# A graph layer's last softmax and tail: four guard passes on ScalarE, reciprocals cut in other pieces, a minimum of negated logits, far rows moved behind the second step's weights, tiles finished one after the other

## What is computed

```python
h = relu(layernorm(x))                                   # x is 256 x 1024
e = relu(concat(h[src], h[dst]) @ W_kind + b_kind)       # 8448 edges, three kinds of edge
logit = (e @ W_a + b_a)[:, 0]
alpha = softmax of logit over the edges with the same dst
z = segment_sum(alpha[:, None] * h[src], dst)
x = x + relu(concat(h, z) @ W_hn + b_hn)   for rows 0..63
x = x + relu(concat(h, z) @ W_on + b_on)   for rows 64..255
h2 = relu(layernorm(x))
out = x + h2 @ W.T + bias      # W: edge_weight added up at (src, dst), only its 256 x 256 corner is not zero
```

## Time and profile before

| | us |
|---|---|
| median of 3 runs (lowest, highest) | 320.19 (319.69, 320.27) |
| the profiled execution, its own time | 319.85 |
| its span in the trace | 317.8 |
| TensorE busy in the span | 306.4 (96%) |
| VectorE, ScalarE busy | 255.8 (81%), 174.4 (55%) |

### The profile page before, as it was taken

How to read it: one execution, slowest core, us unless ns; L and a number is a source line. 1 busy time by engine, 2 the same in 40 slices (tenths; PEclk the granted TensorE clock), 3 DMA queues, 4 the chain that set the end, 5 groups by cost and what they waited for, 6 DMA issues and landing times.

```text
span 317.8 us, 4204 instructions
## 1 busy us (share of the span) xinstructions
PE 306.4 (96%) x1394; PEld 194.1 (61%) x1399; DVE 255.8 (81%) x442; ACT 174.4 (55%) x437; POOL 154.5 (49%) x149
## 2 busy tenths in 40 slices
PE   8899999999979899999999999999999998999995
PEld 3687688656646667566566666575744645456443
DVE  4775448490799999999979999979898798998164
ACT  3892351573067775648966655865338675493102
POOL 3140027305877778778757877468778600000000
PEclk9999999999999999999999999999999999999999
DMA  6999999999999999999999999999999999999604
GB/s 194 418 425 416 399 427 366 419 424 415 402 405 411 410 407 414 411 410 412 419 419 406 413 415 407 418 418 410 413 413 413 411 414 411 395 377 426 244 0 132
DMA packets 29384, 122.04 MB, mean 384 GB/s; under 512 B 3498, under 2 KB 4010, under 8 KB 24628
## 3 DMA queue, kind: packets, MB, share of 16 engines
q0 software_dynamic: 19008, 69.21, 54.5%
q1 hardware_dynamic: 9236, 48.38, 38.1%
q10 hardware_dynamic: 1120, 4.19, 3.2%
HBM read 115.49 MB, written 6.29 MB: 383 GB/s over the span
## 4 chain that ended last, share of the span: by engine, by line
PE 51%; DMA 20%; DVE 10%; POOL 8%; issue 6%; ACT 4%; SPq 0%; DVEq 0%; ACTq 0%; POOLq 0%
PE psG L1086 17%; PE psG L959 14%; DMA Gp<-p_ho,ids 9%; PE psA L996 5%; DMA q_ho<-T 4%; PE psW L996 4%; POOL Gq L428 3%; DMA q_oo<-T 3%; DVE Gp L737 3%; POOL Gp L414 3%; DMA Gq<-q_ho,ids 2%; PE psG L1163 2%; PE psB L996 2%; PE psG L1056 2%; ACT RL L547 2%
## 5 line engine op out<-in xcount | busy, mean ns | idle before, releaser
L1086 PE MATMUL psG<-W,hT 128*128 128x512 f32 x192 | 84.9, 593 | 0.0
L414 POOL DMA_INDIRECT Gp<-p_ho,ids x60 | 64.1, 1068 | 42.5 <-DMA p_ho<-T 21.4
L737 DVE TENSOR_TENSOR Gp<-Gp,Gq 128x1024 f32<-128x1024 f32 x57 | 69.6, 1220 | 16.6 <-DMA Gq<-q_ho,ids 11.1
L428 POOL DMA_INDIRECT Gq<-q_ho,ids x56 | 65.9, 1178 | 31.3 <-issue 16.8
L741 DVE SCALAR_TENSOR_TENSOR Gp<-Gp,wa 128x1024 f32<-128x1024 f32 x65 | 79.2, 1219 | 0.6
L1086 PEld LDWEIGHTS psG<-W,hT 128*128 128x128 f32 x192 | 35.3, 190 | 39.1 <-issue 39.1
L537 ACT ACTIVATE RW<-ohs,ewh 128x256 fp32r<-128x256 f32 x66 | 33.1, 502 | 34.4 <-DVE ohs L728 28.4
L996 PE MATMUL psW<-RW,ohd 128*128 128x256 f32 x264 | 44.2, 290 | 0.0
L996 PE MATMUL psA<-RL,ohd 128*128 128x256 f32 x240 | 35.4, 291 | 4.3 <-ACT RL L547 3.7
L996 PEld LDWEIGHTS psW<-RW,ohd 128*128 128x128 f32 x264 | 36.3, 189 | 2.9 <-issue 2.9
L996 PEld LDWEIGHTS psA<-RL,ohd 128*128 128x128 f32 x240 | 30.4, 189 | 9.3 <-ACT RL L547 8.2
(11 more groups left out here) (187 smaller groups left out, 393.0 us busy)
## 6 DMA issues: line engine op xcount, KB each, us to landing
W<-weights SPq DMA_DIRECT2D x30, 1024.0 KB, 8.5
Gq<-weights SPq DMA_DIRECT2D x2, 1024.0 KB, 9.3
Gp<-weights SPq DMA_DIRECT2D x4, 512.0 KB, 8.7
Gp<-weights SPq DMA_DIRECT2D x2, 1024.0 KB, 11.8
xs<-x SPq DMA_DIRECT2D x4, 256.0 KB, 3.6
W<-weights SPq DMA_DIRECT2D x2, 512.0 KB, 6.7
h_rows<-h SPq DMA_DIRECT2D x1, 1024.0 KB, 9.0
pre_f<-weights SPq DMA_DIRECT2D x1, 1024.0 KB, 9.9
```

What stands on the lines that cost most here:

```text
L414: nc.gpsimd.indirect_dma_start(out=Gp[:, i % NP, :], out_offset=None, in_=p_oo if t <= OO_TILES else p_ho, in_offset=bass.IndirectOffsetOn ...
L428: nc.gpsimd.indirect_dma_start(out=q_place[Q_PLACE[i]], out_offset=None, in_=q_oo if t <= OO_TILES else q_ho, in_offset=bass.IndirectOffse ...
L737: nc.vector.tensor_tensor(Gp[:, i % NP, :], Gp[:, i % NP, :], q_place[Q_PLACE[i]], ALU.add).then_inc(s_sum, 1)
L1086: last = nc.tensor.matmul(psG[:, 2 * t + half, :], hT[:, k, t * P:(t + 1) * P], W[:, s, half * HALF:(half + 1) * HALF], start=u != 1 and k ...
```

## The change

- **Guards.** ScalarE makes a fourth pass, `inv` = -inv - 1, so that it holds the negated count, and VectorE's addition of 1 is gone. `off` gets the opposite sign with a negated bias tile `nbar`, made once at the start. `inv`, `off`, `Z` and `Ex` lie in `few` and `inv_few`, so the passes wait for `few_sums`.
- **Softmax.** `exp_in` takes the minimum of negated values straight into `nm[:, 1]`; the two small operations behind it are gone, and ScalarE works with scale -1 and with `mx` as a bias. Columns 0 to 63 of tile 1's reciprocal come before `exp_in(0)`, 64 to 127 behind it, 128 to 255 behind `alphas(0)` as before.
- **TensorE.** `keep_busy` ahead of `turned(0)` is gone. The eight `sums` lie in two banks and are copied in two passes. The loop of `hn_rows` and `on_rows` starts right behind them, with `turned(1)` inside it; then `far_rows(0)`, `swapped_stats`, `far_rows(1)`. In the tail, transpose and second layer of tile 0 come first, with two and five `keep_busy` matmuls around them, and then those of tile 1.
- **VectorE.** Tile 0's new rows and statistics come first, then tile 1's; tile 0's last addition (L898) stands ahead of both L895.
- **SP's queue.** x is loaded ahead of `brep`, tile 0's three parts first and tile 1 on a semaphore of its own. The order of the stores is as before.

```diff
 
-        _, inv, off, Z, Ex, zT = shared(("gq_low", [P, 1, D], f32), ("inv", [P, NT, N], f32),
-                                           ("off", [P, NT, N], f32), ("Z", [P, NT, N], f32), ("Ex", [P, NT, N], f32),
-                                           ("zT", [P, KC, NH], f32))
+        _, zT = shared(("gq_low", [P, 1, D], f32), ("zT", [P, KC, NH], f32))
         Gq = sb("Gq", [P, NQ, D], f32)
         RW = sb("RW", [P, WRING, 2, N], f32r)
         _, pre_l = shared(("rl_low", [P, D], f32), ("pre_l", [P, 2, D], f32))
@@ -205,9 +203,11 @@
         inv_few = sb("inv_few", [P, 2, NT, N], f32)
         L_few = sb("L_few", [P, 2, NT, N], f32)
         off_few = sb("off_few", [P, 2, NT, N], f32)
+        inv, off = few[:, 0, :, :], few[:, 1, :, :]
+        Z, Ex = inv_few[:, 0, :, :], inv_few[:, 1, :, :]
+        nbar = sb("nbar", [P, 1], f32)
         mx = sb("mx", [P, 2, NT], f32)
         nm = sb("nm", [P, 2, NT], f32)
-        ed = sb("ed", [P, NT], f32)
         fall = sb("fall", [P, NT], f32)
...
             for j in range(KC // 2):
                 load_hn(j)
-            sp.wait_ge(s_used, BREP_AT + 1)
-            sp.dma_start(brep, l1_bias.broadcast_to((P, D))).then_inc(s_lb, 16)
             sp.wait_ge(s_tab[2], 16)
             sp.wait_ge(s_sum, len(GATHERED))
-            sp.dma_start(x1[:, 1, :], x[P:N, :]).then_inc(s_xlo, 16)
             sp.dma_start(x1[:, 0, 0:HALF], x[0:P, 0:HALF]).then_inc(s_xlo, 16)
             for rows, place_of in ((lower, upper), (upper, lower)):
                 sp.dma_start(x1[place_of, 0, HALF:D], x[rows, HALF:D]).then_inc(s_xlo, 16)
+            sp.dma_start(x1[:, 1, :], x[P:N, :]).then_inc(s_xhi, 16)
+            sp.wait_ge(s_used, BREP_AT + 1)
+            sp.dma_start(brep, l1_bias.broadcast_to((P, D))).then_inc(s_lb, 16)
             sp.wait_ge(s_ylo, 1)
             sp.dma_start(out[0:P, N:HALF], x1[:, 0, N:HALF]).then_inc(s_out, 16)
             for rows, place_of in ((lower, upper), (upper, lower)):
...
             nc.scalar.copy(selr[:, :], sel[:, :]).then_inc(s_bh, 1)
+            nc.scalar.activation(nbar[:, :], bar[:, :], ACT.Copy, scale=-1.0).then_inc(s_bh, 1)
             highs(6, KC + 2)
...
             def guard_counts():
 
                 act.wait_ge(s_counted, ET)
-                act.wait_ge(s_sum, FREED_Q + 1)
-                nc.scalar.activation(inv[:, :, :], psC, ACT.Relu, bias=minus[:, 0:1]).then_inc(s_cm, 1)
-                nc.scalar.activation(off[:, :, :], psC, ACT.Relu, bias=unit[:, 0:1], scale=-1.0).then_inc(s_cm, 1)
+                act.wait_ge(s_fewsum, 1)
+                act.wait_ge(s_bh, 3)
+                nc.scalar.activation(inv, psC, ACT.Relu, bias=minus[:, 0:1]).then_inc(s_cm, 1)
+                nc.scalar.activation(off, psC, ACT.Relu, bias=unit[:, 0:1], scale=-1.0).then_inc(s_cm, 1)
                 act.wait_ge(s_cm, 2)
-                nc.scalar.activation(off[:, :, :], off[:, :, :], ACT.Identity, bias=bar[:, 0:1], scale=NEG).then_inc(s_cm, 1)
+                nc.scalar.activation(inv, inv, ACT.Identity, bias=minus[:, 0:1], scale=-1.0).then_inc(s_cm, 1)
+                nc.scalar.activation(off, off, ACT.Identity, bias=nbar[:, 0:1], scale=-NEG).then_inc(s_cm, 1)
 
             def lot_weights(g):
                 if LOTS[g][0] > OO_TILES:
@@ -619,14 +623,16 @@
             nc.scalar.copy(Wd[:, :, :], psW[:, :, :]).then_inc(s_Wd, 1)
             for c in range(NT):
                 act.wait_ge(s_ed, c + 1)
-                nc.scalar.activation(Ex[:, c, :], Z[:, c, :], ACT.Exp, bias=nm[:, 1, c:c + 1]).then_inc(s_ex, 1)
-                nc.scalar.activation(fall[:, c:c + 1], ed[:, c:c + 1], ACT.Exp).then_inc(s_fall, 1)
+                nc.scalar.activation(Ex[:, c, :], Z[:, c, :], ACT.Exp, bias=nm[:, 1, c:c + 1], scale=-1.0).then_inc(s_ex, 1)
+                nc.scalar.activation(fall[:, c:c + 1], nm[:, 1, c:c + 1], ACT.Exp, bias=mx[:, 0, c:c + 1]).then_inc(s_fall, 1)
                 if c == 0:
                     act.wait_ge(s_AT, 1)
                     nc.scalar.copy(AT[:, :, 0:P], psB[:, 1, 0:N].rearrange("p (j n) -> p j n", n=P)).then_inc(s_ATc, 1)
+            for part in range(2):
+                act.wait_ge(s_zT, part + 1)
+                nc.scalar.copy(zT[:, 4 * part:4 * part + 4, :],
+                               (psW[:, 0, :], psB[:, 1, 0:N])[part].rearrange("p (k n) -> p k n", n=NH)).then_inc(s_zTc, 1)
             nc.scalar.activation(warm[:, :], epst[:, :], ACT.Sqrt)
-            act.wait_ge(s_zT, 1)
-            nc.scalar.copy(zT[:, :, :], whole(psW).rearrange("p (k n) -> p k n", n=NH)).then_inc(s_zTc, 1)
             for n, t in enumerate(TAIL):
                 act.wait_ge(s_st2, n + 1)
                 nc.scalar.activation(sd[:, t:t + 1], mv[:, t, 1:2], ACT.Sqrt, bias=epst[:, 0:1]).then_inc(s_sd2, 1)
...
                 chain(nc.vector.tensor_tensor(L_few[:, :, :, :], L_few[:, :, :, :], few[:, :, :, :], ALU.mult))
-                chain(nc.vector.tensor_tensor(A[:, :, :], L_few[:, 0, :, :], L_few[:, 1, :, :], ALU.add))
+                nc.vector.tensor_tensor(A[:, :, :], L_few[:, 0, :, :], L_few[:, 1, :, :], ALU.add).then_inc(s_fewsum, 1)
...
             def exp_in(c):
 
                 chain(nc.vector.tensor_tensor(Z[:, c, :], psA[:, c, :], inv[:, c, :], ALU.mult))
-                chain(nc.vector.tensor_tensor_reduce(out=Z[:, c, :], in0=Z[:, c, :], in1=off[:, c, :], scale=1.0,
-                                                     scalar=mx[:, 0, c:c + 1], op0=ALU.add, op1=ALU.max,
-                                                     accum_out=mx[:, 1, c:c + 1]))
-                nc.vector.tensor_scalar(nm[:, 1, c:c + 1], mx[:, 1, c:c + 1], -1.0, None, ALU.mult)
-                nc.vector.tensor_tensor(ed[:, c:c + 1], mx[:, 0, c:c + 1], mx[:, 1, c:c + 1], ALU.subtract).then_inc(s_ed, 1)
+                nc.vector.tensor_tensor_reduce(out=Z[:, c, :], in0=Z[:, c, :], in1=off[:, c, :], scale=1.0,
+                                                     scalar=nm[:, 0, c:c + 1], op0=ALU.add, op1=ALU.min,
+                                                     accum_out=nm[:, 1, c:c + 1]).then_inc(s_ed, 1)
...
                 nc.vector.tensor_scalar(A[:, c, :], A[:, c, :], den[:, c:c + 1], None, ALU.mult).then_inc(s_alpha, 1)
 
             dve.wait_ge(s_cm, 3)
-            chain(nc.vector.tensor_scalar(inv[:, :, :], inv[:, :, :], 1.0, None, ALU.add))
+            dve.wait_ge(s_ef, 1)
+            dve.wait_ge(s_fewsum, 1)
             inverse(0, 0, N)
+            inverse(1, 0, NH)
+            dve.wait_ge(s_cm, 4)
             dve.wait_ge(s_placed, ET)
             exp_in(0)
-            inverse(1, 0, P)
+            inverse(1, NH, P)
             alphas(0)
             inverse(1, P, N)
             exp_in(1)
             alphas(1)
             dve.wait_ge(s_AT, 2)
             nc.vector.tensor_copy(AT[:, :, P:N], psB[:, 1, N:2 * N].rearrange("p (j n) -> p j n", n=P)).then_inc(s_ATd, 1)
-            dve.wait_ge(s_xlo, 16 * 4)
...
                 nc.vector.scalar_tensor_tensor(out=nb[:, t:t + 1], in0=mv[:, t, 0:1], scalar=-1.0,
                                                in1=rs[:, t:t + 1], op0=ALU.mult, op1=ALU.mult).then_inc(s_nb2, 1)
 
-            new_rows(1, 0)
-            chain(rows_stats(1, 0))
+            dve.wait_ge(s_xlo, 16 * 3)
             for half in range(2):
                 new_rows(0, half)
                 rows_stats(0, half).then_inc(s_stp, 1)
-            new_rows(1, 1)
+            dve.wait_ge(s_xhi, 16)
+            new_rows(1, 0)
+            rows_stats(1, 0)
             dve.wait_ge(s_sts, 1)
             nc.vector.bn_aggr(mv[:, 0, :], psS).then_inc(s_st2, 1)
+            norm2(0, 0)
+            new_rows(1, 1)
             chain(rows_stats(1, 1))
             nc.vector.bn_aggr(mv[:, 1, :], st[:, 1, :, :].rearrange("p b s -> p (b s)")).then_inc(s_st2, 1)
-            for n, t in enumerate(TAIL):
-                norm2(n, t)
+            norm2(1, 1)
+
+            def second_rows(n, t):
+                dve.wait_ge(s_y, n + 1)
+                nc.vector.tensor_tensor(x1[:, t, 0:N], x1[:, t, 0:N], (psW, psA)[t][:, 0, :], ALU.add).then_inc(s_o, 1)
+
+            second_rows(0, 0)
             dve.wait_ge(s_lb, 16)
             for t in TAIL:
                 nc.vector.tensor_tensor(x1[:, t, N:D], x1[:, t, N:D], brep[:, N:D], ALU.add).then_inc(s_ylo, 1)
-            for n, t in enumerate(TAIL):
-                dve.wait_ge(s_y, n + 1)
-                nc.vector.tensor_tensor(x1[:, t, 0:N], x1[:, t, 0:N], (psW, psA)[t][:, 0, :], ALU.add).then_inc(s_o, 1)
+            second_rows(1, 1)
 
         @block.tensor
         def _(pe):
...
                 for j in range(NT):
-                    ins = nc.tensor.matmul(whole(psW)[:, k * NH:(k + 1) * NH], rows_h[:, j, k * P:(k + 1) * P],
+                    ins = nc.tensor.matmul((psW[:, 0, :], psB[:, 1, 0:N])[k // 4][:, k % 4 * NH:(k % 4 + 1) * NH], rows_h[:, j, k * P:(k + 1) * P],
```

(31 more changed lines are left out.)

## The result

The changed kernel took 321.91 us (median of 6 runs, 320.34 to 323.94) against 319.68 us for the kernel before, a ratio of 1.0087 with a 95% interval of 1.0056 to 1.0118: +2.2 us. Forecast were 321.5 and +1.36. The direction was right, the size was not: 0.87% where 0.43% was said. The absolute time is only 0.4 us off because the kernel before came out 0.5 us under the median on record. The profiled execution took 321.78 us with a span of 319.8.

A forecast was written before the change was run, and what follows sets the result against it. Two paths were taken to end together: tile 1's final addition (+0.83 us) and SP's line of six stores (+1.36). The later path sets the end: 320.19 + 1.36, near 321.5 us, range 320.3 to 322.2, slower 0.80.

The forecast's parts named there:

- Guards and softmax: ScalarE's guard passes and the softmax: VectorE's placed logits 0.3 us later, yet `turned(0)` starts 0.13 us sooner.
- TensorE from the sums to `second_bias`: TensorE's reordered list: `sums` 3.8 us, loop 8.74 plus 0.6 for `turned(1)`, all ended at 310.0 against 310.06 before.
- From 306.7 is 309.8, an upper bound for one tile: Tile 0's `h2` done within 3.14 us of 306.7, so `h2_turned(0)` starts at 310.0, 1.43 us sooner.
- rival 4: TensorE's clock falls because `keep_busy` calls are gone; half clock from `turned(0)` on would cost many us; chance 0.01.
- The line of stores: SP's six last stores, released by the first L895, start 1.36 us later and move the end by that; chance 0.61.
- Rival 1: SP's line of stores doesn't bind; the end goes with tile 1's final addition, +0.83 us: 321.0; chance 0.13.
- two paths end together: In the kernel before, tile 1's final addition and the line of stores end together; delaying either moves the end.
- The rule on issuing time: At SP's stores the trace doesn't agree: six issues take 3.27 of the last 5.7 us; the rule would give Rival 1.
- Rivals 2 and 3: 2: `keep_busy` and stores hide in waits, 320.2, chance 0.12. 3: small TensorE matmuls cost no time, -2.1 us, 319.5, chance 0.08.

The follow-up runs named there:

- before_pause: Kernel before without its five `keep_busy` ahead of `h2_turned(0)`; 27.69 us from `turned(0)` to the end, against 26.98 in the kernel before.
- roots_apart: Changed kernel with ScalarE making tile 0's `h2` right behind tile 0's root, ahead of tile 1's root; ratio to the kernel before 1.0090.
- pause_filled: Changed kernel with five more `keep_busy` in front of `h2_turned(0)`, where TensorE was idle; ratio to the kernel before 1.0078.
- no_five: Changed kernel without the five `keep_busy` between tile 0's layer and `h2_turned(1)`; ratio to the kernel before 1.0096.
- tile_by_tile: Changed kernel with ScalarE doing root, `h2` and copy of tile 0, then of tile 1; ratio to the kernel before 1.0015 in the third run.
- bias_first: Changed kernel with both additions of `brep` ahead of tile 0's final addition, as in the kernel before; ratio to the kernel before 1.0056.
- pause_again: Second run of before_pause, the same kernel; 27.52 us from `turned(0)` to the end, against 26.98 in the kernel before.

## Why the prediction was right or wrong, point by point

- **Guards and softmax: right.** VectorE could go on with the placed logits 2.64 us behind its own last logit, against 2.35 before: +0.29, 0.3 forecast. `turned(0)` gained 6.30 - 6.12 = 0.18 on the same scale, 0.13 forecast. The minimum took 0.48 us as the maximum did, and alone the part is neutral (0.9994). x was in time too: VectorE's first new rows of tile 0 waited for TensorE, and came 2.1 us sooner behind `turned(0)` than before (12.30 against 14.40).
- **TensorE from the sums to `second_bias`: right, 0.3 to 0.4 us too dear.** The two halves of `sums` led from 290.49 to the loop in 3.71 us where I had 3.96. Loop with `turned(1)`: 9.25, forecast 9.2. `far_rows` 1.83, `swapped_stats` 0.42: as forecast. `second_bias` ended at about 308.7, 19.1 behind `turned(0)`; I had 19.4.
- **"From 306.7 is 309.8, an upper bound for one tile": the step that failed.** I took the stretch from `far_rows(1)` to both `h2` in the earlier trace rows as a bound and reasoned only with VectorE's order. On ScalarE tile 0's `h2` had to wait for tile 1's root, and the root for VectorE's new rows of tile 1, which wait for the *second* far group. From the end of the first far group (about 305.4) it took 4.8 us, not 3.14. With ScalarE's order mended in full the tail fell from 30.18 to 28.13, and from 29.68 where only the clock was held: 1.55 us for the order.
- **The clock: rival 4, given 1 in 100, was in the profile.** I priced the pause ahead of `turned(0)`, 0.1 to 0.4 us, and not one ahead of `h2_turned(0)`, since the step above had removed it. Cost in the profile 30.18 - 29.68 = 0.50 us. The Trainium skill, TensorE: Matmul & The Clock Gate, section Part 1: The HAM clock gate, has the clock follow the engine's recent activity; before_pause agrees, where it fell 0.5 us behind the end of a pause of 1.30 us.
- **The line of stores: right.** SP's six issues ran without a gap in roots_apart, pause_filled, no_five and tile_by_tile, and the end came 5.6 to 5.7 us behind the first, as it did in the kernel before (5.66) and in the changed one (5.59). Rival 1 is out: no_five's last addition was ready 0.87 us sooner than pause_filled's, and the end didn't move. But "two paths end together" was wrong of the kernel before: its end came 3.44 us behind the start of its last addition, where 2.65 to 2.74 are enough, so that path had 0.7 us or more to spare. before_pause agrees: the addition came 1.47 us later, the end 0.71.
- **The rule on issuing time: not settled.** The Trainium skill, DMA: Bandwidth & Descriptors, section Issuing engines are not separate DMA queues, calls the time to start a transfer usually small beside the transfer. The changed kernel's sixth store was issued 0.4 us late and took 0.33 us of SP's time, against 0.55 in no_five, and the end came no later behind the first store. So the 5.6 us of the line aren't SP's time alone, and no run here separates it from the transfers.
- **The size of the forecast: 0.4 us too dear even for the kernel that I had in mind.** In tails the forecast was 319.2 - 290.7 = 28.5; tile_by_tile has 28.13, and the interval of its time, -0.2 to +1.1 us, leaves out +1.36. Predicted mechanism 28.13 - 26.98 = 1.15, ScalarE's order 1.55, the clock 0.50: together the 3.2 us. That the measured 321.91 falls into the stated range of 320.3 to 322.2 is luck: +2.2 us on the 320.19 on record would be 322.4.
- **Rivals 2 and 3: out.** Moved matmuls kept their time (0.42 for `swapped_stats`, 1.06 for `second_bias` in pause_filled), and ten `keep_busy` took 1.1 us from their start to the next instruction's at full clock.

Open: the times agree with the tails only within about 0.7 us. Less the 0.2 us that `turned(0)` gained, the tails of roots_apart, pause_filled, no_five and bias_first ask for +3.3, +2.5, +2.5 and +1.1 us; the ratios give +2.9, +2.5, +3.1 and +1.8. That the clock falls behind the pause in other executions of no_five and bias_first than the profiled ones would explain their excess, but it wasn't counted over more traces. The clock's 0.50 us rests on single profiles. In the times, of the five edits of the tail that were made to find the cause, only tile_by_tile (1.0015) stands clear of the changed kernel (1.0087).

## What to carry to other kernels

When a change finishes one tile before the next, read the list of every engine on the way, not only of those that the diff touches: a list that goes over both tiles step by step (both roots, both activations, both copies) ties the first tile to the second at each step. Two edits may be needed, and mending one only moves the wait. And once several stores leave one queue at the end, what counts is when the first of them is released; ask which instruction of another engine stands ahead of that release.

## What the runs showed of the hardware that wasn't expected

A pause of TensorE of 1.3 to 1.5 us near the end, in a stretch that is busy otherwise, was followed by a fall of the granted clock from 1.0 to 0.5 in four profiles (changed, roots_apart, before_pause, pause_again), between 0.4 us ahead of the pause's end and 1.3 us behind it, and by none in two (no_five, bias_first) with the same pause. In the eleven profiles without such a pause it didn't fall between `turned(0)` and the last matmul. While it was low, four 256-column matmuls took 1.6 to 2.1 us in place of 1.13, which a granted clock in tenths over 8 us of the page hardly shows: the last digit fell from 9 to 7, but it is 7 for no_five too, where the fall came behind the last matmul. Only windows of one us showed where.
